# A new order of calls on all five engines, with new PSUM banks

## The reference

```python
# layer 0, per sequence
a = x + attention(layernorm(x) @ w_qkv, mask) @ w_ao                 # "self"
b = a + attention(layernorm(a) @ w_q, ctx @ w_kv, mask) @ w_co       # "cross"
c = b + gelu(layernorm(b) @ w1) @ w2                                 # "mlp0"
# layer 1: c is query and, behind the context, also part of keys and values
keys = concat(ctx, c) @ kv_w                                         # "ctx" and "lat"
d = c + attention(c @ q_w, keys, key_mask) @ out_w                   # "lat"
out = c + gelu(rmsnorm(d) @ mlp_w1) @ mlp_w2                         # "mlp1"
```

## Time and profile before

| | |
|---|---|
| median of 3 runs | 1087.88 us (1087.06 to 1089.66) |
| span of the profiled execution | 1086.8 us |
| TensorE matmul busy | 1004.1 us, 92% |
| VectorE busy | 988.4 us, 91% |
| ScalarE busy | 849.4 us, 78% |
| GpSimd busy | 681.9 us, 63% |

### The profile page before, as it was taken

How to read it: one execution, slowest core, us unless ns; L and a number is a source line. 1 busy time by engine, 2 the same in 40 slices (tenths; PEclk the granted TensorE clock), 3 DMA queues, 4 the chain that set the end, 5 groups by cost and what they waited for, 6 DMA issues and landing times.

```text
span 1086.8 us, 46478 instructions
## 1 busy us (share of the span) xinstructions
PE 1004.1 (92%) x19180; PEld 890.8 (82%) x19180; DVE 988.4 (91%) x2328; ACT 849.4 (78%) x1905; POOL 681.9 (63%) x909
## 2 busy tenths in 40 slices
PE   6776989999999999999999999999999999998997
PEld 5665778888888888888888888888888888886786
DVE  4989897999999999999999999999999999988763
ACT  3446789887888888888788888878888888786894
POOL 3777575666666667666667676666676676655221
PEclk9879999999999999999999999999999999999999
DMA  8843112222322222222222222222222222311111
GB/s 275 280 114 74 42 39 41 44 45 58 59 49 51 52 57 43 49 54 58 58 49 45 57 47 48 50 58 58 49 49 54 56 44 49 61 37 37 31 37 36
DMA packets 169700, 67.70 MB, mean 62 GB/s; under 512 B 151184, under 2 KB 167312, under 8 KB 168464
## 3 DMA queue, kind: packets, MB, share of 16 engines
q1 hardware_dynamic: 169488, 64.72, 26.1%
HBM read 26.93 MB, written 4.19 MB: 29 GB/s over the span
## 4 chain that ended last, share of the span: by engine, by line
PE 37%; ACT 26%; DVE 20%; issue 11%; POOL 4%; DMA 2%; SPq 0%; ACTq 0%; POOLq 0%; DVEq 0%
PE psum L457 9%; PE psum L598 7%; PE psum L630 7%; ACT staging L2017 7%; PE psum L470 6%; ACT hid_mlp L2017 6%; PE psum L564 3%; ACT L2003 3%; PE psum L584 3%; DVE mx_lat L1248 3%; ACT L2017 2%; ACT probT_self L2003 2%; DVE late L1267 2%; DVE mx_ctx L1254 2%; DMA turned_mlp<-pair_mlp 1%
## 5 line engine op out<-in xcount | busy, mean ns | idle before, releaser
L2499 POOL TENSOR_TENSOR prob_self<-prob_self,add_self 128x512 f32<-128x512 f32 x64 | 86.8, 1376 | 66.1 <-DVE prob_self L1238 63.4
L2499 POOL TENSOR_TENSOR prob_cross<-prob_cross,add_cross 128x512 f32<-128x512 f32 x64 | 94.5, 1495 | 52.9 <-DVE prob_cross L1238 52.9
L2505 POOL TENSOR_TENSOR late<-late,mx_ctx 128x512 f32<-128x512 f32 x64 | 67.3, 1053 | 86.6 <-DVE mx_ctx L1254 84.1
L2017 ACT ACTIVATE hid_mlp<-psum,folded,undo_in 128x128 f32<-128x128 f32 x256 | 95.6, 455 | 6.9 <-PE psum L457 6.4
L2017 ACT ACTIVATE staging<-psum,cols,undo_in 128x128 f32<-128x128 f32 x256 | 97.4, 481 | 3.3 <-PE psum L457 3.1
L457 PE MATMUL psum<-turned_mlp,hi_n 128*128 128x128 f16 x1024 | 94.2, 221 | 1.6 <-DVE late L1267 1.0
L630 PE MATMUL psum<-hi_n,staging 128*128 128x256 f16 x512 | 94.3, 273 | 1.5 <-DVE staging L1297 1.5
L457 PE MATMUL psum<-turned_mlp,hi_m 128*128 128x128 f16 x1024 | 93.4, 220 | 0.6 <-DMA turned_mlp<-pair_mlp 0.5
L630 PE MATMUL psum<-hi_m,parts_mlp 128*128 128x256 f16 x512 | 89.9, 273 | 1.2 <-DVE xb L1291 0.9
L457 PE MATMUL psum<-turned_mlp,lo_n 128*128 128x128 f16 x512 | 90.3, 221 | 0.0
L457 PE MATMUL psum<-turned_mlp,lo_m 128*128 128x128 f16 x512 | 89.6, 220 | 0.0
(11 more groups left out here) (265 smaller groups left out, 3850.0 us busy)
## 6 DMA issues: line engine op xcount, KB each, us to landing
xin<-in_x SPq DMA_DIRECT2D x32, 128.0 KB, 2.2
late<-in_ctxT SPq DMA_DIRECT2D x4, 1024.0 KB, 5.7
...
```

Source lines behind the costliest of these rows:

```text
L2017: last = e.activation(hid[t][g][:, j * P:(j + 1) * P], ps[:, j * P:(j + 1) * P], ACT.Gelu_apprx_tanh, bias=b1[:, 4 * g + j:4 * g + j + 1], ...
L2499: e.tensor_tensor(ch, ch, over_heads(a[:, :]), ALU.add).then_inc(sem["added_" + t], 1)
L2505: e.tensor_tensor(ch, ch, over_keys(max_of("ctx", h)), ALU.subtract).then_inc(sem["shifted_ctx"], 1)
```

## The change

All five lists are put in a new order, in the prologue, in the loop and in the epilogue, and TensorE's calls are given new PSUM banks. Every call of the kernel before is there once, with the same instructions and the same waits for its operands. The waits for a bank follow the new banks. TensorE's calls keep their lag in units; on the other engines a few calls move over the boundary of a slot and so have another lag in the text (`add_residual(t - 3, "self")` at the slot's head becomes `add_residual(t - 2, "self")` at the end of the one before). The loop of each engine:

```diff
# TensorE, the loop over the slots (before from L816, after from L814)
-prob_turn(t - 6, "lat", 4)
-prob_turn(t - 6, "ctx", 2)
-project(t - 3, "self", 6)
-q_lat(t - 5, 5)
-k_cross(t - 3, 3)
-project(t - 4, "cross", 4)
-v_ctx(t - 5, 1)
-score_bank(t - 5, "ctx", 6)
-score(t - 5, "ctx", 4)
-mix(t - 6, "lat", 2)
-v_lat(t - 5, 6)
+project(t - 3, "self", 4)
+prob_turn_bank(t - 6, "ctx", 5)
+prob_turn_bank(t - 6, "lat", 7)
+prob_turn(t - 6, "lat", 6)
+prob_turn(t - 6, "ctx", 1)
+q_lat(t - 5, 4)
+v_ctx(t - 5, 2)
+project(t - 4, "cross", 7)
+score_bank(t - 5, "ctx", 5)
+score(t - 5, "ctx", 3)
+mix(t - 6, "lat", 1)
 outward(t - 8, "mlp1", 0, 7)
+k_cross(t - 3, 6)
 score_bank(t - 2, "self", 4)
+v_lat(t - 5, 3)
 score(t - 2, "self", 0)
+q_cross(t - 3, 2)
 outward(t - 8, "mlp1", 1, 7)
-q_cross(t - 3, 4)
-k_lat(t - 5, 2)
 hidden(t - 4, "mlp0", 0, 5)
-score_bank(t - 3, "cross", 0)
-score(t - 3, "cross", 6)
-hidden(t - 4, "mlp0", 1, 4)
-hidden(t - 7, "mlp1", 0, 3)
-prob_turn_bank(t - 2, "self", 5)
-prob_turn(t - 2, "self", 1)
-hidden(t - 7, "mlp1", 1, 0)
-k_ctx(t - 4, 2)
-outward(t - 4, "mlp0", 0, 4)
-outward(t - 4, "mlp0", 1, 4)
-prob_turn_bank(t - 3, "cross", 3)
-prob_turn(t - 3, "cross", 0)
+score_bank(t - 3, "cross", 3)
+hidden(t - 4, "mlp0", 1, 2)
+k_lat(t - 5, 0)
+score(t - 3, "cross", 5)
+hidden(t - 7, "mlp1", 0, 7)
+hidden(t - 7, "mlp1", 1, 3)
+outward(t - 4, "mlp0", 0, 1)
+prob_turn_bank(t - 2, "self", 4)
+outward(t - 4, "mlp0", 1, 1)
+prob_turn(t - 2, "self", 2)
+k_ctx(t - 4, 0)
+prob_turn_bank(t - 3, "cross", 7)
+prob_turn(t - 3, "cross", 3)
+score_bank(t - 5, "lat", 4)
 mix(t - 2, "self", 1)
-score_bank(t - 5, "lat", 6)
-score(t - 5, "lat", 4)
+score(t - 5, "lat", 6)
 mix(t - 3, "cross", 0)
-v_cross(t - 2, 3)
-prob_turn_bank(t - 5, "lat", 1)
-project(t - 6, "lat", 2)
+project(t - 6, "lat", 1)
+v_cross(t - 2, 2)
+v_self(t - 1, 3)
 qk_self(t - 1, 0)
-v_self(t - 1, 3)
-prob_turn_bank(t - 5, "ctx", 7)
# VectorE, the loop over the slots (before from L1578, after from L1580)
-q_bias_self(t - 2)
 moments(t - 7, "mlp1")
+moments(t - 3, "cross")
 k_spread(t - 2, "self", 0)
-add_residual(t - 3, "self")
-moments(t - 3, "cross")
+k_spread(t - 2, "self", 1)
+add_residual(t - 4, "cross")
 hidden_lo(t - 8, "mlp1", 0)
-add_residual(t - 4, "cross")
 moments(t - 4, "mlp0")
 masked(t - 5, "ctx", 0)
+low_pair(t - 3, "cross")
+masked(t - 5, "ctx", 1)
+denominators(t - 6, "lat")
+hidden_lo(t - 8, "mlp1", 1)
+divided(t - 6, "lat")
+low_pair(t - 4, "mlp0")
+k_spread(t - 3, "cross", 0)
+k_spread(t - 3, "cross", 1)
+largest_score(t - 5, "ctx", 0)
+masked(t - 2, "self", 0)
+masked(t - 2, "self", 1)
+low_pair(t - 1, "self")
 low_pair(t - 7, "mlp1")
-low_pair(t - 3, "cross")
-k_spread(t - 2, "self", 1)
-masked(t - 5, "ctx", 1)
-low_pair(t - 4, "mlp0")
-hidden_lo(t - 8, "mlp1", 1)
+add_mlp(t - 8, "mlp1")
 moments(t, "self")
-k_spread(t - 3, "cross", 0)
-denominators(t - 6, "lat")
-masked(t - 2, "self", 0)
-divided(t - 6, "lat")
-masked(t - 2, "self", 1)
-k_spread(t - 3, "cross", 1)
 heads_low(t - 6, "lat")
 largest_score(t - 2, "self", 0)
-add_mlp(t - 8, "mlp1")
+largest_score(t - 2, "self", 1)
 k_spread(t - 5, "lat", 0)
-shifted(t - 2, "self", 0)
-largest_score(t - 2, "self", 1)
 k_spread(t - 5, "lat", 1)
-shifted(t - 2, "self", 1)
 masked(t - 3, "cross", 0)
-largest_score(t - 5, "ctx", 0)
 masked(t - 3, "cross", 1)
 hidden_lo(t - 4, "mlp0", 0)
+shifted(t - 2, "self", 0)
+hidden_lo(t - 4, "mlp0", 1)
+shifted(t - 2, "self", 1)
 largest_score(t - 3, "cross", 0)
+largest_score(t - 3, "cross", 1)
+shifted(t - 3, "cross", 0)
+shifted(t - 3, "cross", 1)
+add_mlp(t - 4, "mlp0")
 largest_score(t - 5, "ctx", 1)
-shifted(t - 3, "cross", 0)
-hidden_lo(t - 4, "mlp0", 1)
-largest_score(t - 3, "cross", 1)
-shifted(t - 3, "cross", 1)
-low_pair(t - 1, "self")
-add_mlp(t - 4, "mlp0")
 k_spread(t - 4, "ctx", 0)
 k_spread(t - 4, "ctx", 1)
 lat_low(t - 4)
 denominators(t - 2, "self")
 divided(t - 2, "self")
 largest_score(t - 5, "lat", 0)
+largest_score(t - 5, "lat", 1)
+largest_both(t - 5, 0)
 heads_low(t - 2, "self")
 denominators(t - 3, "cross")
+largest_both(t - 5, 1)
 divided(t - 3, "cross")
-largest_both(t - 5, 0)
-largest_score(t - 5, "lat", 1)
-heads_low(t - 3, "cross")
-largest_both(t - 5, 1)
 shifted(t - 5, "lat", 0)
 shifted(t - 5, "lat", 1)
+heads_low(t - 3, "cross")
 add_residual(t - 6, "lat")
+q_bias_self(t - 1)
+add_residual(t - 2, "self")
# ScalarE, the loop over the slots (before from L2156, after from L2153)
+heads_high(t - 4, "cross")
 values(t - 2, "self")
+values(t - 3, "cross")
 exponential(t - 6, "lat", 0)
 exponential(t - 6, "ctx", 0)
 exponential(t - 6, "lat", 1)
 q_bias_lat(t - 5)
 exponential(t - 6, "ctx", 1)
+normalize(t - 3, "cross")
+hidden_hi(t - 8, "mlp1", 1)
+normalize(t - 4, "mlp0")
 scaled_high(t - 7)
-normalize(t - 3, "cross")
-normalize(t - 4, "mlp0")
 values(t - 5, "ctx")
+heads_high(t - 6, "lat")
 values(t - 5, "lat")
-heads_high(t - 6, "lat")
 q_bias_cross(t - 3)
 gelu(t - 4, "mlp0", 0)
+gelu(t - 4, "mlp0", 1)
 hidden_hi(t - 4, "mlp0", 0)
-gelu(t - 4, "mlp0", 1)
+hidden_hi(t - 4, "mlp0", 1)
 gelu(t - 7, "mlp1", 0)
-hidden_hi(t - 4, "mlp0", 1)
 gelu(t - 7, "mlp1", 1)
 exponential(t - 2, "self", 0)
 exponential(t - 2, "self", 1)
 lat_high(t - 4)
 exponential(t - 3, "cross", 0)
 exponential(t - 3, "cross", 1)
+normalize(t, "self")
 heads_high(t - 2, "self")
-normalize(t, "self")
-heads_high(t - 3, "cross")
-values(t - 2, "cross")
 hidden_hi(t - 7, "mlp1", 0)
-hidden_hi(t - 7, "mlp1", 1)
# GpSimd, the loop over the slots (before from L2634, after from L2637)
 root(t - 7, "mlp1")
 root(t - 3, "cross")
 high_pair(t - 3, "cross")
 root(t - 4, "mlp0")
-high_pair(t - 1, "self")
+plus_bias(t - 4, "mlp0")
 high_pair(t - 4, "mlp0")
-mask_keys(t - 4)
+ctx_high(t - 2)
 added(t - 2, "self", 0)
 added(t - 2, "self", 1)
+mask_add(t - 1)
+ctx_low(t - 2)
 root(t, "self")
-plus_bias(t - 4, "mlp0")
-mask_add(t - 2)
 added(t - 3, "cross", 0)
 added(t - 3, "cross", 1)
-ctx_high(t - 2)
 plus_bias(t - 2, "self")
-plus_bias(t - 4, "lat")
-ctx_low(t - 2)
-plus_bias(t - 3, "cross")
 shifted_ctx(t - 5, 0)
 plus_bias(t - 5, "mlp1")
+plus_bias(t - 4, "lat")
 shifted_ctx(t - 5, 1)
+plus_bias(t - 3, "cross")
+mask_keys(t - 3)
+high_pair(t, "self")
# SyncE, the loop over the slots (before from L2899, after from L2896)
 load_x(t)
-load_rest(t - 2)
+heads_across(t - 7, "lat")
+heads_across(t - 3, "self")
+across(t - 5, "lat")
+heads_across(t - 4, "cross")
+load_rest(t - 1)
 across(t - 3, "cross")
 across(t - 4, "mlp0")
 across(t - 7, "mlp1")
-heads_across(t - 6, "lat")
 store(t - 10)
 across(t - 1, "self")
-across(t - 4, "lat")
-heads_across(t - 2, "self")
-heads_across(t - 3, "cross")
```

Of the prologue, the opening as an example (ScalarE and SyncE); the rest of prologue and epilogue is reordered in the same manner:

```diff
# ScalarE
 squares_of(0, "qkv")
 normalize(0, "self")
+normalize(1, "self")
 high_weight(0, "qkv")
 high_rest(0, "qkv")
 squares_of(0, "q")
-normalize(1, "self")
 high_side(0, "out")
...
# SyncE
-load_x(0)
 load_weight(0, "qkv")
 load_columns(0)
-load_x(1)
+load_x(0)
 load_tile(0, "side")
+load_x(1)
 load_tile(0, "out")
 load_weight(0, "q")
+load_x(2)
 across(0, "self")
...
```

More of the change, by code:

```diff
@@ L737, in _ @@
[L737 removed]
+            prob_turn_bank(0, "cross", 1)
+            prob_turn(2, "self", 3)
+            v_self(3, 6)
+            project(1, "self", 3)
+            qk_self(3, 4)
+            prob_turn(0, "cross", 7)
+            mix(2, "self", 4)
+            mix(0, "cross", 3)
+            score_bank(3, "self", 6)
+            score(3, "self", 1)
+            total(0, "n1", 0)
+            k_cross(1, 6)
+            q_cross(1, 7)
+            project(0, "cross", 5)
+            score_bank(1, "cross", 3)
@@ new lines, in _ @@
+            v_cross(1, 6)
+            score(1, "cross", 1)
+            k_ctx(0, 7)
+            v_ctx(0, 3)
+            prob_turn_bank(3, "self", 5)
+            project(2, "self", 0)
+            qk_self(4, 2)
+            prob_turn(3, "self", 0)
+            k_cross(2, 4)
+            score_bank(4, "self", 5)
+            score(4, "self", 2)
+            hidden(0, "mlp0", 0, 1)
+            mix(3, "self", 5)
+            v_self(4, 0)
+            prob_turn_bank(1, "cross", 1)
+            through(0, "lo", 7)
@@ new lines, in _ @@
+            mix(5, "self", 0)
+            prob_turn_bank(1, "lat", 3)
+            prob_turn(1, "lat", 4)
+            hidden(3, "mlp0", 0, 1)
+            score_bank(4, "cross", 5)
+            score(4, "cross", 2)
+            hidden(3, "mlp0", 1, 7)
+            hidden(0, "mlp1", 0, 4)
+            mix(1, "lat", 3)
+            score_bank(2, "ctx", 1)
+            k_lat(2, 6)
+            q_lat(2, 5)
+            v_ctx(2, 3)
+            hidden(0, "mlp1", 1, 4)
+            score(2, "ctx", 6)
@@ new lines, in _ @@
+            prob_turn_bank(UNITS - 6, "lat", 5)
+            prob_turn(UNITS - 6, "lat", 6)
+            prob_turn(UNITS - 6, "ctx", 1)
+            q_lat(UNITS - 5, 2)
+            k_cross(UNITS - 3, 4)
+            project(UNITS - 4, "cross", 5)
+            mix(UNITS - 6, "lat", 7)
+            score_bank(UNITS - 5, "ctx", 5)
```

(5 more changed lines are left out.)

1374 lines of the change are left out of this document (660 added, 714 removed).

## The result

The changed kernel takes 1165.62 us (median of 4 runs, 1162.58 to 1167.05) beside 1088.69 for the kernel before (4 runs). The ratio is 1.071, 95% interval 1.069 to 1.073. I forecast 1069, range 1056 to 1086: wrong in sign, by 97 us.

The account below looks back on a forecast made before the run. A ring through TensorE and VectorE set the 30.89 us slot; TensorE's floor was 29.66. New slot 29.72 + 0.15 (across lat) + 0.25 (late heads, stretches) = 30.1, saving 19 us over 24 slots: 1069 us, range 1056 to 1086.

Parts of the forecast that it names:

- VectorE's own sum: VectorE's work per steady slot: 29.6 us with the stretches left in, no more than TensorE needs.
- the stretches of the old order: Near the slot's end on VectorE, `heads_pair_cross` and the second `mx_ctx` run longer, costing 0.47 + 0.52 us.
- Rival 2: VectorE becomes the bound: heads_low self held 0.47 us by GpSimd's shift each slot, slot 30.57, 1080 us; chance 0.15.
- Rival 3: Slower: the heads' transpose lands late as a rule for TensorE's self project, ring 31.4, 1101 us; chance 0.08.
- The old ring: Old slot's loop: TensorE 24.83 us from late's transposes through self mix, VectorE 5.68, hand-overs 0.12 and 0.14, together 30.77.
- my rings: Three rings of the new steady slot, at 29.5 to 29.8 us; likeliest slot 29.8 to 30.4.
- What is late next: Self heads' DMA transpose must land before TensorE's self project, now first in its slot; ring 29.72 us, no cushion.
- late heads and stretches: Allowance of 0.25 us a slot for late landings of heads and stretched VectorE calls.
- Filling and draining: Opening and closing outside the 24 slots: taken as 0, with 6 us either way.
- Chances: Odds given for the whole change: faster 0.85, same 0.06, slower 0.09.

Follow-up runs that it names:

- with small and with scalar additions: Two runs, changed kernel with GpSimd's mask additions cut to 8 keys per head, 1104.6 us; or made as tensor_scalar additions of 0, 1116.19 us.
- the reverse experiment: Kernel before with two VectorE calls moved, divided(lat) behind masked(self, 1) and masked(cross, 1) behind two largest_score calls: 1148.56 us.
- VectorE's order alone: Changed kernel with 21 of VectorE's 58 calls of a slot moved, no other engine touched: 1107.27 us, ratio 1.016 to the kernel before.
- the last run: Kernel before with divided(cross) on VectorE behind largest_both(0) and plus_bias(mlp1) on GpSimd behind shifted_ctx(1): 1072.33 us, ratio 0.983.
- the run with one move: Kernel before with one VectorE call moved, masked(cross, 1) behind two largest_score calls: 1118.79 us, ratio 1.024.

## Why the prediction was wrong, step by step

- **The step that failed: VectorE's own sum.** I took "29.6 with the stretches left in", that is, the stretches of the old order, and added none for new neighbours. Measured, the new order adds 4.0 us a slot: 29.6 + 4.0 = 33.6, and the slot is 33.75. The step failed in that it took each call's duration as fixed, where it hangs on what GpSimd does beside it. The runs with other VectorE orders, with small and with scalar additions, and the reverse experiment on the kernel before each move the time with these calls. I had read the mechanism in the earlier trace rows and named it, but tried it on one pair only, `heads_low(self)` beside GpSimd's first shift. That one was never held (0.42 us in both). GpSimd's four mask additions, its costliest calls, were in none of my rows.
- **Rival 2 was of the right kind and an eighth of the size**: it held one call by 0.47 us and gave 1080. Rival 3 was the wrong mechanism for the sign: `heads_turned_self` costs 3.5 us in 3 slots.
- **The old ring** was right. The 0.78 us wait of L584 on `late` is gone, and with most of the stretches gone half of the slots were 30.6 (VectorE's order alone), where my rings allowed 29.8 to 30.4. But that the old ring "closes to the hundredth" proves nothing: four steps between starts, laid end to end over one slot, always add up to the slot. What bears it out are the waits at both hand-overs, and the last run, in which a shorter VectorE part of the ring made the slot 30.09.
- **What is late next** named the wrong transfer. Self heads and `turned_lat` cost 5.9 us over the slots, less than I priced them (0.15 a slot for `turned_lat` and 0.25 for late heads and stretches, 9.6 together). `turned_mlp`, which I had not priced, costs 19.2.
- **Filling and draining**: within 6 us I said; the opening is 14.3 longer, the closing stretch 4.3 shorter, together 10.0. I looked at loads and ScalarE and never laid the engines' openings beside each other. In the changed kernel TensorE's busy time is 2.39 of the 5 us ahead of 30 us and all 10 of 30 to 40, there at a granted clock of 0.52, nearly all at the lower of its two levels (1.2 and not 2.4 GHz), with 69 matmuls, while GpSimd does nothing; the kernel before had 0.97, 149 matmuls and all engines at work. That low clock alone is not the cause: with the loads in the old order the clock from 30 to 40 us is 1.00 (the low stretch, 0.52, lies at 25 to 30), and unit 0 still starts at 61.0. Restoring the early order alone gains nothing.
- **Chances**: 0.09 on slower was too little. VectorE was 97% busy, so most of what made an operation of it longer had to show in the time (1.60 us of stretch made the slot 1.16 longer in the run with one move), and I looked at one.

A rule of the Trainium skill bears on this twice. The page "SBUF — State Buffer", section "SBUF: two separate sides", says that of a VectorE operation with two SBUF inputs and a GpSimd operation that reads SBUF, whichever starts first holds the pair of ports for the whole instruction. By that rule, the trace agrees for GpSimd's tensor_tensor on 128x256 and 128x512: what is left, less 0.13 to 0.20 us. With GpSimd's tensor_scalar on 128x512 in SBUF the trace disagrees: `prob_self` at 680 ns and `pair_mlp` at 473 are not held. Nor is `pair_mlp` (477 ns in the kernel before) when a 128x1 power of GpSimd, also a tensor_tensor, has 0.39 us left. The measurement decides, for these shapes.
